# Sorting batches of a graph kernel: five of sixteen tiles scattered by GpSimd and eleven placed by TensorE, instead of three and thirteen

## The reference

```python
row, col = edge_index[0], edge_index[1]            # src, dst
messages = jnp.einsum('ei,oi->eo', x[col], W) + b
out = jax.ops.segment_sum(messages * agg_weight, row, num_segments=x.shape[0])
x = _layernorm(x + out, axis=-1)
```

## Time and profile before

| what | us |
|---|---|
| median of three runs | 838.07 (833.6 to 838.79) |
| span of the profiled execution | 834.4 |
| of it, up to the first `own` of the sorting loop | 49.5 |
| of it, from there to the last placing matmul | 213.4 |
| of it, the decode and the main stage | 571.5 |

### The profile page before, as it was taken

One profiled execution on the slowest core, in us unless ns is written; L12 is line 12 of the kernel. 1 busy time (PEld: TensorE's weight loads), 2 busy tenths in 40 slices (PEclk: granted clock), 3 DMA queues, 4 the chain that ended last, 5 costly groups with the idle time before them and its releaser, 6 DMA issues.

```text
span 834.4 us, 23648 instructions
## 1 busy us (share of the span) xinstructions
PE 756.2 (91%) x8073; PEld 550.6 (66%) x8073; DVE 769.2 (92%) x2547; ACT 660.2 (79%) x1659; POOL 494.7 (59%) x510
## 2 busy tenths in 40 slices
PE   4889999999999978999998899999999999899894
PEld 3844555555554656777777777777777777677773
DVE  7989999999998788999999999998999999999995
ACT  2157878787885368899888889888889888888898
POOL 2024333333421777777777777777777777777750
PEclk9999999999999999999999999999999999999998
DMA  2001110111113257888777788777777878778773
GB/s 78 2 27 40 28 40 28 32 36 28 41 35 103 61 177 223 246 243 254 235 253 232 238 241 247 246 237 235 233 248 245 254 234 248 228 251 252 232 240 135
DMA packets 78148, 139.46 MB, mean 167 GB/s; under 512 B 16864, under 2 KB 17900, under 8 KB 78028
## 3 DMA queue, kind: packets, MB, share of 16 engines
q1 hardware_dynamic: 62476, 110.50, 39.5%
q0 software_dynamic: 15552, 27.43, 14.4%
HBM read 86.04 MB, written 51.83 MB: 165 GB/s over the span
## 4 chain that ended last, share of the span: by engine, by line
PE 37%; DVE 27%; issue 13%; DMA 8%; POOL 7%; ACT 7%; ACTq 0%; POOLq 0%; SPq 0%; DVEq 0%
PE bank L737 10%; DMA xg<-in_x,table 8%; POOL xg L527 7%; PE bank L660 5%; DVE stats L1002 4%; DVE oh_s L891 4%; DVE sel L986 3%; ACT y L1109 3%; PE bank L707 3%; PE bank L711 3%; PE bank L709 3%; DVE oh_t L893 3%; DVE rest L984 3%; DVE xl L989 2%; PE bank L553 2%
## 5 line engine op out<-in xcount | busy, mean ns | idle before, releaser
L527 POOL DMA_INDIRECT xg<-in_x,table x417 | 415.7, 997 | 147.5 <-issue 100.3
L1109 ACT ACTIVATE y<-h,shift,rstd 128x128 f32<-128x128 f32 x784 | 321.6, 482 | 24.5 <-DVE shift L1013 24.4
L737 PE MATMUL bank<-wT,aggT 128*128 128x128 f32 x1568 | 229.0, 290 | 0.0
L737 PEld LDWEIGHTS bank<-wT,aggT 128*128 128x128 f32 x1568 | 191.6, 193 | 27.4 <-issue 10.8
L709 PE MATMUL bank<-sel,rest 128*128 128x385 bf16 (+25 forms) x708 | 183.7, 261 | 0.0
L707 PE MATMUL bank<-sel,xg 128*128 128x385 bf16 (+25 forms) x708 | 176.6, 262 | 3.2 <-DVE xl L989 3.0
L711 PE MATMUL bank<-sel,xl 128*128 128x385 bf16 (+25 forms) x708 | 174.9, 261 | 0.0
L479 POOL DMA_INDIRECT place_scratch<-word_col,place_row x69 | 71.6, 1038 | 131.3 <-DVE place_row L882 108.0
L1002 DVE BATCH_NORM_STATS2 stats<-h 128x6 f32<-128x256 f32 x392 | 148.0, 418 | 0.2
L995 DVE TENSOR_TENSOR h<-bank,xt 128x512 f32<-128x512 f32 x196 | 133.7, 682 | 5.9 <-PE bank L737 5.1
L660 PE MATMUL bank<-oh_t,oh_s 128*128 128x417 bf16 x644 | 129.0, 345 | 6.2 <-ACT oh_s L1073 0.8
(11 more groups left out here) (156 smaller groups left out, 743.1 us busy)
## 6 DMA issues: line engine op xcount, KB each, us to landing
xt<-in_x SPq DMA_DIRECT2D x195, 256.0 KB
out<-y SPq DMA_DIRECT2D x195, 256.0 KB
xg<-in_x,table POOLq DMA_INDIRECT x417
hi_row<-hi_scratch SPq DMA_DIRECT2D x50, 128.0 KB
place_scratch<-word_col,place_row POOLq DMA_INDIRECT x69
place_scratch<-scattered SPq DMA_DIRECT2D x1, 417.0 KB, 3.5
scattered<-place_scratch SPq DMA_DIRECT2D x1, 417.0 KB, 3.2
src_rows<-in_src SPq DMA_DIRECT2D x1, 192.0 KB
```

The lines of the kernel that those rows point to most:

```text
L527: nc.gpsimd.indirect_dma_start(out=xg[:, m, k], out_offset=None, in_=x, in_offset=bass.IndirectOffsetOnAxis(ap=table[:, period * LISTS + k ...
L737: last = nc.tensor.matmul(OUT[u % RO][:, nodes[j]], aggT[:, u % RO, nodes[j]], wT[:], start=False, stop=True, skip_group_check=True)
L1109: nc.scalar.activation(y[:, u, j], h[:, u, j], ACT.Identity, bias=shift[:, u, j:j + 1], scale=rstd[:, u, j:j + 1]).then_inc(s_y, 1)
```

## The change

For batches 0 to 21, 11 tiles are placed and 5 are scattered; batch 22 keeps 13 and 3, and the last two are as they were. That makes 278 tiles placed and 113 scattered. `SCATTERS`, the shares of `part_of` (for 11 tiles 2, 3 and 6; for 13 they are 3, 3 and 7) and POOL's loop `range(BY_PE[k], BC)` follow from the list.

```diff
-    BY_PE = [13] * (B - 3) + [13, BC, C - (B - 1) * BC]
+    BY_PE = [11] * (B - 3) + [13, BC, C - (B - 1) * BC]
```

## The result

| | us |
|---|---|
| before, median of four runs | 836.54 (833.6 to 838.79) |
| after, median of four runs | 823.01 (820.92 to 824.87) |
| ratio | 0.983, 95% interval 0.981 to 0.986 |
| span of the profiled execution | 834.4 before, 823.1 after |

The account below looks back on a forecast made before the run. The prediction took the sorting stage's PE-ACT loop (8.51 us a batch) as the bound; 1.6 + 0.35 + 20 x 0.645 + 0.355 = 15.2 us, and 838.07 - 15.2 = 822.9, said as 823, range 817 to 830 us.

Parts of the forecast that it names:

- The loop that bounds: Sorting stage, 8.51 us a batch: PE's third share saves 0.355 us, ACT's first share 0.29 us, giving 7.86 us.
- DVE and POOL costed at nothing: Sorting loop: DVE's wait before `own` grows to nearly 0.8 us, POOL keeps 1.3 us idle; added scatters cost nothing.
- A: Rival in the sorting stage: POOL's scatters become the bound; at a pitch of 2.0 us, 858 us; chance 0.05.
- The sum: Gain over the sorting stage: 1.6 + 0.35 + 20 x 0.645 + 0.355 = 15.2 us.
- The first batches: Start of the sorting loop, DVE-bound before the second `own`: reciprocal 1.6 us earlier, next batch gains about 0.35 us.
- TensorE's clock: PE in the sorting loop: full 2.4 GHz even at 48 to 52 us, so no matmul priced at 1.2 GHz.
- Behind the loop: Decode and main stage: scatter table stays early (12.9 us before), same instructions start earlier; forecast difference 0.
- rival C: Main stage of gathers, loads and stores gives back gain, say 9 us: about 832 us; chance 0.05.
- B: Rival in the sorting loop: DVE's tiles release the first share, third share off the loop; 8.3 us, about 830; chance 0.08.
- D: Rival in the sorting loop: more gain, with DVE as floor at 7.2 us a batch; about 820 to 817; chance 0.04.

## Why the prediction was right

The forecast was 823 us, the median is 823.01. By its own steps:

**The loop that bounds.** Right. PE's third share and ACT's first share are the loop, not the chain's DVE tiles: the kernels with shares 3, 3, 6 and 2, 3, 7 show each term alone (0.36 and 0.30 us for 0.355 and 0.29), and the kernel without scatters the sum (7.85 us for 7.86). My reason to put the wait in the code above the releaser named by the chain holds.

**DVE and POOL costed at nothing.** Right: DVE waits 0.7 to 1.1 us before `own` in the changed kernel, POOL 1.3 to 1.8 us before a batch's first scatter, and thirteen tiles with five scatters have the old period. No scatter is stretched; the summary of L479 after answers to the earlier trace rows:

```profile
L479 POOL DMA_INDIRECT place_scratch<-word_col,place_row x113: 962/1046/1179, 50.8 to 231.5; - x113
```

Its median fell from 1089 to 1046 ns and its longest is 1179 ns as before, so the trap of the Trainium skill (SBUF — State Buffer, its box on the "DVE blocks DMA" trap) does not show in this kernel. Whether its VectorE instructions run in a two-port mode, no run shows. The decision to price A by the rows' pitch stands.

**A term left out.** The sum was 15.2 us, and the loop gave 12.2 us (213.42 us from first `own` to decode, then 201.20). Missing are 2.3 us in the 20 batches, since 11 of them have a copy 0.24 us late beside a scatter, and 0.7 us in the first ones (next point). I had looked for what a scatter does to DVE and not for what it may do to a signal from PE to ACT, and the rows of before had no scatter in that place: its first scatter started 0.30 us ahead of `prefix` (122.67 against 122.97), and in the changed kernel 0.06 us behind it, because the shorter third share brings `prefix` forward and `place_row` does not move with it.

**The first batches.** The term of 1.95 us was 1.3 us between the two profiles. The reciprocal came 1.4 us earlier behind the first `own` (8.47 us, then 7.09) for the 1.6 of the sum. The batch after it took 8.01 us in this execution and 7.22 us in the second profile of the same kernel, where first to third `own` took 17.83 us, 2.05 less than before. So the term is about right, and what spoiled it here is TensorE's clock.

**TensorE's clock.** This step was wrong, and in this execution it cost the sum 0.8 us. I took a granted clock of 1.00 at 48 to 52 us as proof that PE keeps 2.4 GHz with little to do. Windows of 52 to 56 us, before and after, the pair L609 in them, and 64 to 68 us of the changed kernel:

```profile
52.00:56.00 4.00, 3.91 (x26) 1.63 (x27) 4.00 (x18) 3.16 (x8) 3.19 (x3) 1.00 0.01 1
...
54.84 0.61 PE L609 MATMUL bank<-age_col,age_row 32*128 32x512 bf16 x2
```

```profile
52.00:56.00 4.00, 4.00 (x28) 1.74 (x26) 3.85 (x15) 3.43 (x10) 2.98 (x3) 0.50 0.02 1
...
64.00:68.00 4.00, 4.00 (x38) 2.19 (x39) 2.96 (x14) 3.33 (x10) 2.92 (x3) 0.64 0.03 3
...
52.85 0.61 PE L609 MATMUL bank<-age_col,age_row 32*128 32x512 bf16 x2
```

The same two matmuls take 0.61 us in both, and 0.39 us later on (the row at 101.37 above). The placing matmuls (L660) say the same: between 53 and 56 us they start 0.35 us apart in both executions, and 0.178 us in the regular batches, at a granted clock of 1.00. So PE ran at 1.2 GHz there in both executions, and the column says so only in one. That distance is the evidence that I should have named for 2.4 GHz in the batches. The clock also fell again after the start of the loop: from 58 to 64 us PE had 4.58 us of work in 6, and from 64 to 68 us the mean granted clock is 0.64. That is the batch of 8.01 us; the four profiles with the shares of 2, 3 and 6 that read 1.00 there have 7.22 or 7.23 us for it.

**Behind the loop.** The stage from the decode to the end was costed at no change and took 2.2 us more. In the 14 profiled executions of this study, all with the same instructions there, it takes from 569.0 to 574.9 us, so 2.2 us between two profiles say little. But the medians say more. They differ by 13.5 us on the first chip and by 10.3 us on the one where the changed kernel was run again, while its loop was 13.4 us shorter than before. Of the eleven comparisons of kernels with a whole output, the first has 1.3 us more between the medians than between the loops of the profiles, and the ten others have 1.3 to 3.8 us less (the loop of before is taken from its one profile). The largest of these is the kernel before with two more scatters a batch, slower by 3.7 us with the same loop. So a part of rival C seems real, about 2 us, and that last kernel speaks against its reason: there the main stage starts at the same time as before. What the scatters leave behind for it is open.

So the hit to the tenth is luck. The size is the loop's 12.2 us where 15.2 was said. The rest is spread: of the start (1.3 us), of the main stage (2.2 us the other way), and of the runs before, whose median came down from 838.07 to 836.54 us with a fourth run. The rivals: B fell (shares 3, 3, 6), A is real but needs seven scatters (nine tiles), C has perhaps 2 us of the 9 that it was given, and D did not occur here; ten tiles go further by a shorter share and not by a hidden gap. D's own figure was not worked out to its end, either: a fifth of 13 us is 2.6 us, which gives 820 and not 817.

## What to carry to other kernels

In a loop that two engines hand to and fro, follow the waits in the code around one period and price only what stands between two of them; a busy share of 92% (DVE) can still be off the loop, and the chain's releaser can be an engine that had long been done. Work that an idle engine does "for free" is free for the loop until its own pitch times its count passes the deadline of whoever collects it: write that as one sum (here start + count x pitch + read back) and it gives the turning point before any run. When a share gets shorter, list what now falls beside each start on the loop; moving the scatters by one wait was worth as much as a third of a tile a batch.

## What the runs showed of the hardware that was not expected

- A signal from PE to ACT can come 0.24 us late when POOL starts an indirect DMA about 0.5 us before it is due, though PE's next matmul is not late: 11, 9 and 4 of 20 batches with five, five and three scatters a batch, none without scatters or with the scatter behind the copy. With four scatters (shares 3, 3, 6) in the same place it is none of 19, and one of one with the scatter 0.1 us before the signal is due. It is 0.03 us late in every batch with shares 3, 3, 5, where the scatter starts 0.2 us ahead of the copy. What decides is open.
- Scatters issued without a wait for `place_row` between them come 1.27 us apart at the shortest and 1.30 us in the mean (nine tiles).
- The granted clock of a profile can read 1.00 where the matmuls' lengths and distances say half (0.61 for 0.39 us, 0.35 for 0.178 us).
- A stage with the same instructions differs by up to 1% (569.0 to 574.9 us) between kernels that differ only ahead of it. One kernel with an unchanged loop and 44 more scatters ahead of that stage was measured 0.5% (0.3 to 0.7%) slower than before. The cause is open.
